# The value product of a retention layer, computed with tokens in the rows of y

## The chip, the cores and the metric

The kernel runs on one core of a Trainium2 chip. The metric is the device time of one launch in microseconds; lower is better. Engines are called as in the profile: PE is TensorE (its matmuls), PEld its weight loads, DVE VectorE, ACT ScalarE, POOL GpSimd, SP the engine that issues DMAs. TensorE multiplies a stationary operand, which a weight load puts into its array, by a moving operand that is streamed through it. In the calls below the order of arguments is (output, stationary, moving): the stationary operand's columns become the output's rows, the moving operand's columns the output's columns.

## The reference

For every sequence of 1,024 tokens (8 of them, 256 features) a retention layer and a quantised feed-forward layer are added to the input. The changed lines lie in the retention layer (`_xpos` is a rotary encoding; 8 heads of 32 features):

```python
xn = _layernorm(x)
Q = _xpos(jnp.einsum('bse,hed->bhsd', X, W_Q))
K = _xpos(jnp.einsum('bse,hed->bhsd', X, W_K), downscale=True)
V = jnp.einsum('bse,hed->bhsd', X, W_V)
scores = jnp.einsum('bhsd,bhtd->bhst', Q, K) * D[None]   # D: causal decay gam**(s-t)
Y = jnp.einsum('bhst,bhtv->bhsv', scores, V)
Yn = ((Y - mu) / jnp.sqrt(var + EPS)).reshape(b, s, h * dv) * gn_weight + gn_bias  # per head
gate = X @ W_G; gate = gate * sigmoid(gate)
retention = gate * Yn @ W_O
# feed-forward: fp4 blocks of 16; silu(xq @ w_gate.T) * (xq @ w_up.T), quantised, @ w_down.T
out = x + retention + ffn
```

## The kernel before

The 8,192 tokens are worked off in 64 tiles of 128 tokens, 8 tiles to a sequence. Within a sequence the scores of a tile reach only the tile's own tokens; what earlier tiles contribute is carried in `state` (K transposed times V, summed up), kept for all tiles but the last of a sequence (`kept(t)`; `later(t)` is true for all but the first).

Every engine runs one instruction stream, written out by hand. `step(i)` is the loop body of each engine, i from -4 to 65; in it the engine works on tile i for the projections and the scores, on tile i-1 for the second half of its feed-forward part and y's norm, on tile i-2 for the last pieces and the output, and on tiles i+1 to i+3 for the layer norm and quantisation of the input. Engines meet only in semaphores, and none overtakes within its own stream. So the code's order in a step is the order in time.

What the change and the prediction touch, by name and line of the profile:

- PE, late in step i: three transposes of `hq` (L883), then for kept tiles `kv`, K transposed times V of tile i (L892, eight small products, one a head), then the value product (L901, eight, one a head, val stationary: 32 columns, probs moving: 128), which fills `b_yT`, features in the rows, tokens in the columns. Then the feed-forward's down product (L908, L912, L913). Ahead of L901, for tiles with a state, `state` times `qT` (L869) starts the same sums. L844 is the product of K and Q that makes the scores, eight heads of 32 rows. fp32 products show two records each, one transpose shows one.
- PE, early in step i+1: the query and key projection (L773 to L775, "bank"), the rest of the down product (L789 to L792), the output product of z (L795, L796: high part of z; L808: its low part), and between them the transposes of yT (L802), which turn y to tokens in the rows. After L808 come the gate and up products, dense and long (L773 to L775, "quad").
- ACT, at the end of step i: the copy of yT out of PSUM (L725), then `h_magic` (L727). In step i+1 the state's copies for kept tiles (L672, four), `zT_hi` (L677), the squares of y (L681), `x_magic`.
- POOL, first in a step: `zT_lo` (L376), the low part of z, which L808 waits for (semaphore `z_low`).
- DVE: the sums of squares (L548), the scaled `y_hat` (L592), and the masked scores `probs` (L600, L603). L544 adds L808's result to the input.

Of the kernel before, what the change touches and what calls it, by code (L numbers as in the profile page):

```python
# [19 lines left out]
G = 2  # L20
# [40 lines left out]
def block_kernel(nc, x, w_q, w_k, w_v, w_g, w_o, gn_w, gn_b, w_gate, w_up, w_down, cos_d, sin_d,  # L61
# [4 lines left out]
    with ExitStack() as ctx:  # L66
        def sb(name, shape, dt=F32):
            return ctx.enter_context(nc.sbuf_tensor(name, shape, dt))

        def sem(name):  # L70
            return ctx.enter_context(nc.semaphore(name))
# [54 lines left out]
        probs = sb("probs", [P, HG, G * P])  # L126
        state_sum = sb("state_sum", [P, G * HD])
        state = sb("state", [P, D])
        yT = sb("yT", [P, D])
        y_sq = sb("y_sq", [P, D])  # L130
        y_hat = sb("y_hat", [P, D])
        u_T = sb("u_T", [P, KD, P])
# [28 lines left out]
        b_kv = bank[3]  # L161
        b_out = bank[4][:, 0:D]
        b_vg = bank[6]
        b_yT = [bank[5][:, 0:P], bank[6][:, 0:P]]
        b_y = b_zT = bank[7]


        w_landed = [sem(f"w_landed{n}") for n in range(len(PARTS))]
# [78 lines left out]
        xT_high = sem("xT_high")  # L247
        affine1 = sem("affine1")
        hT_high1 = sem("hT_high1")
        yT_copy = sem("yT_copy")  # L250
        h_abs = sem("h_abs")


        qk_ready = sem("qk_ready")
        down_l1 = sem("down_l1")
        out_high = sem("out_high")
        y_ready = sem("y_ready")
        out_ready = sem("out_ready")
        gu0_ready = sem("gu0_ready")
        gu1_ready = sem("gu1_ready")  # L260
# [7 lines left out]
        down_h0 = sem("down_h0")  # L268
        h1_turned = sem("h1_turned")
        kv_ready = sem("kv_ready")  # L270
        yT_ready = sem("yT_ready")
        down_l0 = sem("down_l0")
        down_h1 = sem("down_h1")

        def exists(t):
            return 0 <= t < TILES
# [18 lines left out]
        def heads(ap):  # L295
            return ap.rearrange("p (h d) -> p h d", d=HD)
# [4 lines left out]
        def tiles(ap):  # L301
            return ap.rearrange("p (k c) -> p k c", c=P)

        def spread(ap, k=BLOCK):
            return ap.unsqueeze(2).broadcast_to([P, ap.shape[1], k])
# [129 lines left out]
        def _(dve):  # L435
# [68 lines left out]
            def step(i):  # L504
# [84 lines left out]
                if exists(i - 1):  # L589
                    t = i - 1  # L590
                    dve.wait_ge(rstd_ready, t + 4)
                    dve.tensor_tensor(heads(y_hat[:]), heads(b_y[:, 0:D]), spread(rstd[:, 1:], HD), ALU.mult).then_inc(y_normed, 1)  # L592
                if exists(i):
                    t = i
                    dve.wait_ge(h_peak, t + 1)
# [67 lines left out]
        def _(act):  # L663
            def step(i):
                if exists(i - 1) and kept(i - 1):
                    t = i - 1
                    if t == 0:
                        act.wait_ge(cleared, 3)
                    act.wait_ge(kv_add, kept_upto(t))
                    for r in range(HG):  # L670
                        rows = slice(r * HD, (r + 1) * HD)
                        ins = act.activation(tiles(state[:])[rows, :, rows], heads(state_sum[:])[rows], ACT.Copy)  # L672
                    ins.then_inc(state_copy, 1)
                if exists(i - 2):
                    t = i - 2
                    act.wait_ge(z_mul, t + 1)
                    act.activation(zT_hi[:], zT[:], ACT.Copy).then_inc(z_high, 1)  # L677
                if exists(i - 1):
                    t = i - 1
                    act.wait_ge(y_ready, t + 1)  # L680
                    act.activation(y_sq[:], b_y[:, 0:D], ACT.Square, scale=HD ** -0.5).then_inc(squared, 1)  # L681
                if exists(i + 1):
                    t = i + 1
                    act.wait_ge(x_divided, t + 1)
                    act.activation(x_magic[:], x_quot[:], ACT.Abs, scale=GROW).then_inc(x_abs, 1)  # L685
                if exists(i):
                    t = i
                    act.wait_ge(gu0_ready, t + 1)
                    act.activation(silu[:, 0, :], b_gate[0][:, 0:FH], ACT.Silu).then_inc(silu0_done, 1)  # L689
                    act.wait_ge(gu1_ready, t + 1)  # L690
                    act.activation(silu[:, 1, :], b_gate[1][:, 0:FH], ACT.Silu).then_inc(silu1_done, 1)  # L691
                    act.wait_ge(qk_turned, t + 1)
                    act.activation(qT[:], tiles(b_qkT[:, 0:D]), ACT.Copy).then_inc(q_copy, 1)
                    act.activation(kT[:], tiles(b_qkT[:, D:2 * D]), ACT.Copy).then_inc(k_copy, 1)
                    act.wait_ge(vg_ready, t + 1)
                    act.activation(val[:], b_vg[:, 0:D], ACT.Copy).then_inc(v_copy, 1)
                if exists(i + 2):
                    t = i + 2
                    act.wait_ge(x_shifted, t + 1)
                    act.activation(xn[:, t % 2, :], x_in[:, t % SLOTS, :], ACT.Identity,  # L700
                                   bias=x_shift[:], scale=rstd[:, 0:1]).then_inc(x_normed, 1)
                if exists(i):
                    t = i
                    act.activation(gate[:, t % 2, :], b_vg[:, D:2 * D], ACT.Silu).then_inc(gate_silu, 1)
                if exists(i - 1):
                    t = i - 1
                    act.wait_ge(h0_turned, t + 1)
                    act.activation(hT_hi[:, 0:3, :], tiles(b_hT[0][:, 0:3 * P]), ACT.Copy).then_inc(hT_high0, 1)
                    act.wait_ge(z_turned, t + 1)
                    act.activation(u_T[:, 0, :], b_zT[:, 0:P], ACT.Identity,  # L710
                                   bias=gnb[:, 0:1], scale=gnw[:, 0:1]).then_inc(affine0, 1)
                if exists(i + 1):
                    t = i + 1
                    act.wait_ge(x_turned, t + 1)
                    act.activation(xT_hi[:], tiles(b_xT), ACT.Copy).then_inc(xT_high, 1)
                if exists(i - 1):
                    t = i - 1
                    act.activation(u_T[:, 1, :], b_zT[:, P:2 * P], ACT.Identity,
                                   bias=gnb[:, 1:2], scale=gnw[:, 1:2]).then_inc(affine1, 1)
                    act.wait_ge(h1_turned, t + 1)  # L720
                    act.activation(hT_hi[:, 3:6, :], tiles(b_hT[1][:, 0:3 * P]), ACT.Copy).then_inc(hT_high1, 1)
                if exists(i):
                    t = i
                    act.wait_ge(yT_ready, t + 1)
                    act.activation(tiles(yT[:]), quad[:, 3:5, 0:P], ACT.Copy).then_inc(yT_copy, 1)  # L725
                    act.wait_ge(h_divided, t + 1)
                    act.activation(h_magic[:], h_quot[:], ACT.Abs, scale=GROW).then_inc(h_abs, 1)  # L727

# [42 lines left out]
        def _(pe):  # L771
# [5 lines left out]
            def step(i):  # L777
# [7 lines left out]
                if exists(i - 2):  # L785
# [9 lines left out]
                        pe.matmul(b_out, zT_hi[:, k], w_out_hi[:, k], start=False, stop=False)  # L795
                        ins = pe.matmul(b_out, zT_hi[:, k], w_out_lo[:, k], start=False, stop=False)  # L796
                    ins.then_inc(out_high, 1)
                if exists(i - 1):
                    t = i - 1
                    pe.wait_ge(yT_copy, t + 1)  # L800
                    for g in range(G):
                        ins = pe.transpose(b_y[:, g * P:(g + 1) * P], yT[:, g * P:(g + 1) * P], ident[:])  # L802
                    ins.then_inc(y_ready, 1)
                if exists(i - 2):
                    t = i - 2
                    pe.wait_ge(z_low, t + 1)
                    for k in range(KD):
                        ins = pe.matmul(b_out, zT_lo[:, k], w_out_hi[:, k], start=False, stop=k == KD - 1)  # L808
                    ins.then_inc(out_ready, 1)
                if exists(i):  # L810
# [9 lines left out]
                        pe.wait_ge(w_low, sum(PART_GROUPS[:-1]))  # L820
                    if t >= 2:
                        pe.wait_ge(summed, t - 1)
                    for dst, c in ((b_gate[1], FH), (b_up[1], F + FH)):
                        for k in range(KD):
                            ins = product(dst[:, 0:FH], xT_hi[:, KD:], xT_lo[:, KD:], w_gu_hi[:, :, c:c + FH],
                                          w_gu_lo[:, :, c:c + FH], k, start=k == 0, stop=k == KD - 1)
# [37 lines left out]
                if exists(i) and later(i):  # L864
                    t = i
                    pe.wait_ge(masked1, t + 1)
                    pe.wait_ge(gate_silu, t + 1)
                    for g in range(G):
                        ins = pe.matmul(b_yT[g], state[:, g * P:(g + 1) * P], qT[:, g, :], start=True, stop=False)  # L869
                    ins.then_inc(st_ready, 1)  # L870
                if exists(i - 1):
                    t = i - 1
# [22 lines left out]
                if exists(i):  # L895
                    t = i
                    pe.wait_ge(gate_silu, t + 1)
                    for g in range(G):
                        for r in range(HG):
                            rows, head = slice(r * HD, (r + 1) * HD), (g * HG + r) * HD  # L900
                            ins = pe.matmul(b_yT[g][rows, :], val[:, head:head + HD], probs[:, r, g * P:(g + 1) * P],  # L901
                                            start=t % CHUNKS == 0, stop=True)
                    ins.then_inc(yT_ready, 1)
                if exists(i - 1):
                    t = i - 1
                    pe.wait_ge(hT_low0, t + 1)
# [71 lines left out]
```

## Time and profile before

| | |
|---|---|
| median of 3 runs | 949.45 us (949.44 to 951.26) |
| the profiled execution's own time | 948.74 us |
| its span (first to last instruction) | 946.9 us |
| PE busy | 888.8 us, 94% |
| DVE busy | 895.9 us, 95% |
| ACT busy | 528.5 us, 56% |
| POOL busy | 443.7 us, 47% |

The span is the profiled execution from its first to its last instruction; 1.8 us of its time lie outside. Two engines are busy nearly throughout. Since matmuls are pipelined, a busy PE says little by itself: how far apart its instructions start has to be read from the timeline. A wait names the engine's instruction that stood idle and who released it.

### The profile page before, as it was taken

Reading aid. Unit: us, or ns where it says so; the run is one execution under the profiler, and the core shown is the slowest. Engines: PE = TensorE matmul, PEld = TensorE weight load, DVE = VectorE, ACT = ScalarE, POOL = GpSimd, SP = SyncE. Lnnn points to the kernel's source line nnn. Section 1 sums busy time; section 2 is a strip of 40 time slices with the busy share of each in tenths; the row PEclk is TensorE's granted clock in tenths of the full one; section 3 lists DMA queues with packets and bytes.
Section 4 is the critical chain, followed back from the end, with each engine's and each line's share of the span. In section 5 each row is a group of like instructions: output and inputs, shape, how many; then the busy total and the mean of one; then the engine's idle time right before and its main releaser. Section 6 shows DMA issues by size and latency. Waiting matters only on the chain.

```text
span 946.9 us, 21085 instructions
## 1 busy us (share of the span) xinstructions
PE 888.8 (94%) x8258; PEld 798.1 (84%) x8258; DVE 895.9 (95%) x2220; ACT 528.5 (56%) x1331; POOL 443.7 (47%) x343
## 2 busy tenths in 40 slices
PE   0169999999999999999999999999999999999997
PEld 0158988898989899889988998998899889989986
DVE  5899999999999999999999999999999999999995
ACT  1345565556556655665555566556655655565553
POOL 3564544553454445444544444554445344444543
PEclk9999999999999999999999999999999999999999
DMA  9000000000000000000000000000000000000000
GB/s 281 40 1 12 24 12 24 23 24 13 24 23 19 18 24 24 12 24 24 24 12 24 24 19 17 23 24 12 24 23 24 14 24 23 18 19 24 12 7 17
DMA packets 28259, 24.95 MB, mean 26 GB/s; under 512 B 9088, under 2 KB 27648, under 8 KB 27904
## 3 DMA queue, kind: packets, MB, share of 16 engines
q1 hardware_dynamic: 20224, 18.95, 6.5%
q10 hardware_dynamic: 7936, 4.66, 1.7%
q8 instruction: 65, 1.06, 0.5%
q14 instruction: 34, 0.28, 0.1%
HBM read 15.21 MB, written 8.39 MB: 25 GB/s over the span
## 4 chain that ended last, share of the span: by engine, by line
PE 91%; DVE 5%; POOL 2%; ACT 1%; DMA 0%; issue 0%; SPq 0%; DVEq 0%; POOLq 0%
PE quad L775 11%; PE quad L773 11%; PE quad L774 11%; PE quad L844 4%; PE quad L908 4%; PE bank L850 3%; PE bank L855 3%; PE quad L901 3%; PE bank L774 3%; PE bank L775 3%; PE bank L773 3%; PE bank L830 3%; PE bank L862 3%; PE quad L869 3%; PE quad L878 2%; PE quad L877 2%
## 5 line engine op out<-in xcount | busy, mean ns | idle before, releaser
L392 POOL TENSOR_TENSOR h_quot<-h,h_inv 128x704 f32<-128x704 f32 x64 | 88.9, 1389 | 266.2 <-DVE h_inv L607 266.2
L388 POOL TENSOR_TENSOR rstd<-var_eps,power 128x9 f32<-128x9 f32 x67 | 158.0, 2358 | 38.6 <-DVE var_eps L557 38.5
L774 PE MATMUL quad<-w_gu_lo,xT_hi 128*128 128x352 f32 x512 | 165.1, 322 | 0.0
L775 PE MATMUL quad<-w_gu_hi,xT_lo 128*128 128x352 f32 x512 | 165.1, 322 | 0.0
L773 PE MATMUL quad<-w_gu_hi,xT_hi 128*128 128x352 f32 x512 | 165.0, 322 | 0.0
L376 POOL TENSOR_TENSOR zT_lo<-zT,zT_hi 128x256 fp32r<-128x256 f32 x64 | 51.8, 809 | 164.6 <-ACT zT_hi L677 164.6
L775 PEld LDWEIGHTS quad<-w_gu_hi,xT_lo 128*128 128x128 f32 x512 | 96.2, 188 | 0.0
L773 PEld LDWEIGHTS quad<-w_gu_hi,xT_hi 128*128 128x128 f32 x512 | 96.2, 188 | 0.0
L774 PEld LDWEIGHTS quad<-w_gu_lo,xT_hi 128*128 128x128 f32 x512 | 96.1, 188 | 0.0
L384 POOL TENSOR_TENSOR qk<-qk_cos,qk_sin 128x512 f32<-128x512 f32 x64 | 82.9, 1295 | 7.1 <-DVE qk_sin L531 6.5
L689 ACT ACTIVATE silu<-quad 128x352 f32<-128x352 f32 x64 | 29.8, 465 | 92.2 <-PE quad L775 92.2
L691 ACT ACTIVATE silu<-quad 128x352 f32<-128x352 f32 x64 | 29.7, 463 | 92.2 <-PE quad L775 92.2
L681 ACT ACTIVATE y_sq<-bank 128x256 f32<-128x256 f32 x64 | 24.6, 385 | 76.2 <-PE bank L802 76.2
L672 ACT ACTIVATE state<-state_sum 32x64 f32<-32x64 f32 x224 | 56.1, 250 | 2.0
L588 DVE TENSOR_REDUCE h_max<-h 128x44 f32<-128x704 f32 x64 | 56.7, 886 | 0.1
L568 DVE TENSOR_TENSOR hq<-h_grid,h_scale 128x704 f32<-128x704 f16 x64 | 56.3, 880 | 0.1
L560 DVE SCALAR_TENSOR_TENSOR h_grid<-h_magic,h_diff 128x704 f16<-128x704 bf16 x64 | 56.1, 877 | 0.0
L773 PE MATMUL quad<-w_qkvg_hi,xT_hi 128*128 128x512 f32 x128 | 55.8, 436 | 0.0
L518 DVE SCALAR_TENSOR_TENSOR h_diff<-h_magic,h_quot 128x704 f32<-128x704 bf16 x64 | 54.8, 856 | 0.8 <-ACT h_magic L727 0.7
L844 PEld LDWEIGHTS quad<-qT,kT 32*128 32x128 f32 x1024 | 34.3, 185 | 24.5 <-issue 24.5
L877 PE MATMUL quad<-w_dn_hi,hT_hi 128*128 128x256 f32 x192 | 54.0, 310 | 0.0
L552 DVE SCALAR_TENSOR_TENSOR x_diff<-x_magic,x_quot 128x256 f32<-128x256 bf16 x64 | 51.1, 799 | 0.8 <-ACT x_magic L685 0.8
(147 smaller groups left out, 2849.5 us busy)
## 6 DMA issues: line engine op xcount, KB each, us to landing
x_in<-in_L_attn_X_dram SPq DMA_DIRECT2D x64, 128.0 KB, 2.1
out_dram<-y_out SPq DMA_DIRECT2D x64, 128.0 KB, 1.7
sin<-const_sin_dram ACTq DMA_DIRECT2D x1, 2048.0 KB, 11.1
cos<-const_cos_dram ACTq DMA_DIRECT2D x1, 1024.0 KB, 6.4
raw<-in_L_ffn_w_down_dram SPq DMA_DIRECT2D x2, 352.0 KB, 4.0
raw<-in_L_ffn_w_gate_dram SPq DMA_DIRECT2D x1, 512.0 KB, 3.9
raw<-in_L_ffn_w_up_dram SPq DMA_DIRECT2D x1, 384.0 KB, 5.4
w_qkvg<-in_L_attn_W_Q_dram ACTq DMA_DIRECT2D x2, 128.0 KB, 5.0
```

Source lines behind the costliest of these rows:

```text
L384: pool.tensor_tensor(qk[:], qk_cos[:], qk_sin[:], ALU.add).then_inc(rope_add, 1)
L388: pool.tensor_tensor(rstd[:], var_eps[:], power[:], ALU.pow).then_inc(rstd_ready, 1)
L392: pool.tensor_tensor(blocks(h_quot[:]), blocks(h[:]), spread(h_inv[:]), ALU.mult).then_inc(h_divided, 1)
L560: dve.scalar_tensor_tensor(h_grid[:], h_magic[:], LEAST, h_diff[:], ALU.max, ALU.subtract).then_inc(h_gridded, 1)
L568: dve.tensor_tensor(blocks(hq[:, 0:F]), blocks(h_grid[:]), spread(h_scale[:]), ALU.mult)
L588: dve.tensor_reduce(h_max[:], blocks(h[:]), AX_X, ALU.max, apply_absolute_value=True).then_inc(h_peak, 1)
L672: ins = act.activation(tiles(state[:])[rows, :, rows], heads(state_sum[:])[rows], ACT.Copy)
L773: pe.matmul(out, hi[:, k], w_hi[:, k], start=start, stop=False)
L774: pe.matmul(out, hi[:, k], w_lo[:, k], start=False, stop=False)
L775: return pe.matmul(out, lo[:, k], w_hi[:, k], start=False, stop=stop)
L844: ins = pe.matmul(quad[:, r, g * P:(g + 1) * P], kT[rows, g, :], qT[rows, g, :], start=True, stop=True)
L877: pe.matmul(b_out, hT_hi[:, k], w_dn_hi[:, k], start=k == 0, stop=False)
```

## The change

The value product L901 changes its operands' places: the masked scores of a head, `probs` (128 keys by 128 queries), become the stationary operand, and `val` (128 keys by 32 features) the moving one, so the output has tokens in the rows and the head's 32 features in the columns. The state's product L869 changes places too (`qT` stationary, `state` moving; both are 128x128). ACT's copy L725 then writes y as the norm wants it, in SBUF. The two transposes of yT (L802) and their semaphore go; the squares and `y_hat` read the copy in SBUF instead of PSUM. In a sequence's first tile, where no state product starts the sum, the first head's product does it. The second half of the gate and up products waits for the copy explicitly, since it writes over bank 5. Operands stay fp32.

```diff
-        yT = sb("yT", [P, D])
+        y = sb("y", [P, D])
...
-        b_yT = [bank[5][:, 0:P], bank[6][:, 0:P]]
-        b_y = b_zT = bank[7]
+        b_yg = [bank[5][:, 0:P], bank[6][:, 0:P]]
+        b_zT = bank[7]
...
-                    dve.tensor_tensor(heads(y_hat[:]), heads(b_y[:, 0:D]), spread(rstd[:, 1:], HD), ALU.mult).then_inc(y_normed, 1)
+                    dve.tensor_tensor(heads(y_hat[:]), heads(y[:]), spread(rstd[:, 1:], HD), ALU.mult).then_inc(y_normed, 1)
...
-                    act.wait_ge(y_ready, t + 1)
-                    act.activation(y_sq[:], b_y[:, 0:D], ACT.Square, scale=HD ** -0.5).then_inc(squared, 1)
+                    act.wait_ge(y_copy, t + 1)
+                    act.activation(y_sq[:], y[:], ACT.Square, scale=HD ** -0.5).then_inc(squared, 1)
...
-                    act.wait_ge(yT_ready, t + 1)
-                    act.activation(tiles(yT[:]), quad[:, 3:5, 0:P], ACT.Copy).then_inc(yT_copy, 1)
+                    act.wait_ge(y_ready, t + 1)
+                    act.activation(tiles(y[:]), quad[:, 3:5, 0:P], ACT.Copy).then_inc(y_copy, 1)
...
-                if exists(i - 1):
-                    t = i - 1
-                    pe.wait_ge(yT_copy, t + 1)
-                    for g in range(G):
-                        ins = pe.transpose(b_y[:, g * P:(g + 1) * P], yT[:, g * P:(g + 1) * P], ident[:])
-                    ins.then_inc(y_ready, 1)
-                if exists(i - 2):
-                    t = i - 2
                     pe.wait_ge(z_low, t + 1)
...
                         pe.wait_ge(summed, t - 1)
+                    if t >= 1:
+                        pe.wait_ge(y_copy, t)
...
-                        ins = pe.matmul(b_yT[g], state[:, g * P:(g + 1) * P], qT[:, g, :], start=True, stop=False)
+                        ins = pe.matmul(b_yg[g], qT[:, g, :], state[:, g * P:(g + 1) * P], start=True, stop=False)
...
-                            rows, head = slice(r * HD, (r + 1) * HD), (g * HG + r) * HD
-                            ins = pe.matmul(b_yT[g][rows, :], val[:, head:head + HD], probs[:, r, g * P:(g + 1) * P],
-                                            start=t % CHUNKS == 0, stop=True)
-                    ins.then_inc(yT_ready, 1)
+                            head = slice((g * HG + r) * HD, (g * HG + r + 1) * HD)
+                            ins = pe.matmul(b_yg[g][:, r * HD:(r + 1) * HD], probs[:, r, g * P:(g + 1) * P], val[:, head],
+                                            start=t % CHUNKS == 0 and r == 0, stop=r == HG - 1)
+                    ins.then_inc(y_ready, 1)
```

The rows that follow give PE's instructions in program order (line, operation, output<-operands, shape of the output, what it waits for). The first place is the end of a step, on PE, for a tile with a state, before:

```order
L883 MATMUL quad<-ident,hq 128x128 [waits masked0]
L883 MATMUL quad<-ident,hq 128x128 x2
L892 MATMUL quad<-val,qk 32x32 [waits masked0,v_copy]
L892 MATMUL quad<-val,qk 32x32 x7
L901 MATMUL quad<-probs,val 32x128 [waits gate_silu]
L901 MATMUL quad<-probs,val 32x128 x7
L908 MATMUL quad<-w_dn_hi,hT_lo 128x256 [waits hT_low0]
L908 MATMUL quad<-w_dn_hi,hT_lo 128x256 x2
```

The same place of the changed kernel, whose line numbers are lower by 7 here:

```order
L876 MATMUL quad<-ident,hq 128x128 [waits masked0]
L876 MATMUL quad<-ident,hq 128x128 x2
L885 MATMUL quad<-val,qk 32x32 [waits masked0,v_copy]
L885 MATMUL quad<-val,qk 32x32 x7
L894 MATMUL quad<-val,probs 128x32 [waits gate_silu]
L894 MATMUL quad<-val,probs 128x32 x7
L901 MATMUL quad<-w_dn_hi,hT_lo 128x256 [waits hT_low0]
L901 MATMUL quad<-w_dn_hi,hT_lo 128x256 x2
```

Nothing moved there; the output's shape went from 32x128 to 128x32. The second place is the next step's first part, on PE, from the output product of z to the gate product, before:

```order
L795 MATMUL quad<-w_out_hi,zT_hi 128x256 [waits z_high]
L796 MATMUL quad<-w_out_lo,zT_hi 128x256
L795 MATMUL quad<-w_out_hi,zT_hi 128x256
L796 MATMUL quad<-w_out_lo,zT_hi 128x256
L802 MATMUL bank<-ident,yT 128x128 [waits yT_copy]
L802 MATMUL bank<-ident,yT 128x128
L808 MATMUL quad<-w_out_hi,zT_lo 128x256 [waits z_low]
L808 MATMUL quad<-w_out_hi,zT_lo 128x256
L773 MATMUL quad<-w_gu_hi,xT_hi 128x352 [waits kv_add]
```

And of the changed kernel (one line lower at its start, nine at L808):

```order
L794 MATMUL quad<-w_out_hi,zT_hi 128x256 [waits z_high]
L795 MATMUL quad<-w_out_lo,zT_hi 128x256
L794 MATMUL quad<-w_out_hi,zT_hi 128x256
L795 MATMUL quad<-w_out_lo,zT_hi 128x256
L799 MATMUL quad<-w_out_hi,zT_lo 128x256 [waits z_low]
L799 MATMUL quad<-w_out_hi,zT_lo 128x256
L772 MATMUL quad<-w_gu_hi,xT_hi 128x352 [waits kv_add]
```

The two transposes between the high and the low part of z's product are gone, so the instruction that waits for `z_low` comes directly behind the high part.

## Rows read from the trace of the kernel before

**Rows 1.** The page: busy time of each engine, granted clock in 40 slices, chain by engine.
```profile
PE 888.8 (94%) x8258; PEld 798.1 (84%) x8258; DVE 895.9 (95%) x2220; ACT 528.5 (56%) x1331; POOL 443.7 (47%) x343
...
PEclk9999999999999999999999999999999999999999
...
PE 91%; DVE 5%; POOL 2%; ACT 1%; DMA 0%; issue 0%; SPq 0%; DVEq 0%; POOLq 0%
```

**Rows 2.** The waits: engine, line, for whom; us in total, times, longest us.
```profile
ACT y_sq L681 <- PE bank L802: 76.2, 63, 2.2
...
PEld quad L908 <- issue: 12.5, 63, 0.2
```

**Rows 3.** Timeline around tile 33: start us, us, engine, line, operation, count [idle before].
```profile
519.62 0.49 PE L883 MATMUL quad<-ident,hq 128*128 128x128 f32 x3
...
520.04 0.33 PE L892 MATMUL quad<-val,qk 128*32 128x32 f32 x16
...
520.16 0.38 PEld L901 LDWEIGHTS quad<-probs,val 128*32 128x32 f32 x16
520.19 0.62 PE L901 MATMUL quad<-probs,val 128*32 128x128 f32 x16
...
520.74 0.41 PEld L908 LDWEIGHTS quad<-w_dn_hi,hT_lo 128*128 128x128 f32 x3 [0.20 <-issue]
...
520.88 0.39 ACT L725 ACTIVATE yT<-quad 128x256 f32<-128x256 f32 x1 [0.24 <-PE quad L901]
...
521.16 0.78 ACT L727 ACTIVATE h_magic<-h_quot 128x704 bf16<-128x704 f32 x1
...
521.84 1.04 ACT L672 ACTIVATE state<-state_sum 32x64 f32<-32x64 f32 x4
...
522.90 0.42 ACT L677 ACTIVATE zT_hi<-zT 128x256 fp32r<-128x256 f32 x1
...
523.40 0.74 POOL L376 TENSOR_TENSOR zT_lo<-zT,zT_hi 128x256 fp32r<-128x256 f32 x1 [2.76 <-ACT zT_hi L677]
...
523.87 0.28 PE L796 MATMUL quad<-w_out_lo,zT_hi 128*128 128x256 f32 x1
...
523.99 0.38 PE L802 MATMUL bank<-ident,yT 128*128 128x128 f32 x2
...
524.19 0.30 PEld L808 LDWEIGHTS quad<-w_out_hi,zT_lo 128*128 128x128 f32 x2
```

**Rows 4.** Timeline of the same stretch around tile 31, the last of its sequence.
```profile
492.55 0.49 PE L883 MATMUL quad<-ident,hq 128*128 128x128 f32 x3
...
492.97 0.65 PE L901 MATMUL quad<-probs,val 128*32 128x128 f32 x16
...
493.55 0.41 PEld L908 LDWEIGHTS quad<-w_dn_hi,hT_lo 128*128 128x128 f32 x3 [0.20 <-issue]
...
495.13 1.32 POOL L376 TENSOR_TENSOR zT_lo<-zT,zT_hi 128x256 fp32r<-128x256 f32 x1 [1.55 <-ACT zT_hi L677]
...
496.93 0.30 PEld L808 LDWEIGHTS quad<-w_out_hi,zT_lo 128*128 128x128 f32 x2
```

**Rows 5.** Timeline, weight loads alone, of three lines around tile 33.
```profile
516.53 0.54 PEld L844 LDWEIGHTS quad<-qT,kT 32*128 32x128 f32 x16 [0.36 <-issue]
...
518.35 0.53 PEld L869 LDWEIGHTS quad<-qT,state 128*128 128x128 f32 x4
...
520.04 0.22 PEld L892 LDWEIGHTS quad<-val,qk 128*32 128x32 f32 x16 [0.17 <-issue]
```

**Rows 6.** Groups by line and form, PE matmuls: busy us, mean ns of one.
```profile
L901 PE MATMUL quad<-probs,val 128*32 128x128 f32 x1024 | 40.1, 274 | 0.0
...
L892 PE MATMUL quad<-val,qk 128*32 128x32 f32 x896 | 18.6, 201 | 1.1 <-DVE probs L603 1.1
```

**Rows 7.** Groups by line and form, PE weight loads: busy us, mean ns of one.
```profile
L869 PEld LDWEIGHTS quad<-qT,state 128*128 128x128 f32 x224 | 29.4, 191 | 0.1
...
L901 PEld LDWEIGHTS quad<-probs,val 128*32 128x32 f32 x1024 | 24.5, 111 | 1.3 <-issue 1.3
```

More of the change, by code:

```diff
@@ L249, in block_kernel @@
         hT_high1 = sem("hT_high1")
-        yT_copy = sem("yT_copy")
+        y_copy = sem("y_copy")
         h_abs = sem("h_abs")
@@ L256, in block_kernel @@
         out_high = sem("out_high")
-        y_ready = sem("y_ready")
         out_ready = sem("out_ready")
@@ L270, in block_kernel @@
         kv_ready = sem("kv_ready")
-        yT_ready = sem("yT_ready")
+        y_ready = sem("y_ready")
         down_l0 = sem("down_l0")
```

## The prediction

> **What bounds the kernel now.** I began with the page: PE and DVE are both busy for some 95% of the span, the clock is granted in full in every slice, and the chain that ended last is 91% on PE [rows 1]. So what PE starts later, the end gets later, unless a wait absorbs it. The waits show hardly any of PE's but gaps of 0.2 us ahead of L908, 63 times, put down to "issue" [rows 2]: nothing released them. The timeline shows why PE is nonetheless not alone. After the value product L901 (last end 520.19 + 0.62 = 520.81) ACT works in one stretch: the copy of yT, h_magic, four copies of the state, zT_hi, up to 523.32; then POOL makes zT_lo, up to 524.14; and L808's weight load starts at 524.19 [rows 3]. PE had started its second transpose of L802 at 523.99 + 0.38 - 0.27 = 524.10 and would have been free to load then: it waits 0.09 us for `z_low` already. So for each tile with a state there are two loops through L808: PE's own instructions, and L901's end, then ACT, then POOL. The second is the longer one, by that 0.09 us. For the last tile of a sequence the state's copies are missing; there POOL is done at 496.45 and L808 loads only at 496.93 [rows 4]: PE alone binds.
>
> **The gap of 0.2 us.** The last matmul of L901 starts at 520.81 - 0.27 = 520.54, L908's load at 520.74 [rows 3]. L883's last starts at 519.62 + 0.49 - 0.27 = 519.84, L892's load at 520.04 (0.17 us idle ahead of it) [rows 3, 5]. Between L892 and L901 there is none: their loads start at 520.04 and 520.16. The array's shape tells them apart: 128*128, 128*32, 128*32, 128*128. A change of shape costs some 0.20 us from the last matmul's start to the next load. The Trainium skill, TensorEngine Tiling, section Tiling Modes, says that changing the tiling mode drains the engine; by that rule the trace agrees.
>
> **The new value product.** Before: 16 records (each fp32 product has two) in 0.62 us; they start (0.62 - 0.27) / 15 = 23 ns apart, since four heads lie side by side in the array, 32 columns each, and run abreast [rows 3]. After: each head takes all 128 columns, nothing runs abreast, and 16 loads of 128 columns must pass, each before a stream of only 32 columns. No row shows this pairing, so I bound the spacing. The nearest for the load is L869, fp32, whole array: loads (0.53 - 0.19) / 3 = 113 ns apart [rows 5], but it also streams 128 columns, which could be what spaces them. That the load itself takes so long: one lasts 191 ns with 128 columns and 111 ns with 32 [rows 7], 80 ns for 96 columns, so 128 take about 107 ns of a port, the rest being latency. L844's loads start in packs of four over four row groups, (0.54 - 0.19) / 3 = 0.12 us a pack [rows 5]; each row group takes a 128-column load as often as that, not oftener. Upper bounds: load and stream one after the other, 27 ns more (the stream of 32 columns, a quarter of 107); or nothing overlaps, the load's full 191 ns. Lower bounds: stream-bound, as in L892, whose 16 loads of 32 columns take (0.22 - 0.11) / 15 = 7 ns each and thus about 30 ns in each of four column groups [rows 5, 7]. I take 112 ns, since L869 is fp32, of the same shape, and one load behind the other is what the durations say.
>
> The Trainium skill, TensorE: Matmul & The Clock Gate, section LDWEIGHTS, has a load take its columns / 1.2 in ns, whatever its rows: 107 ns. The sum by it would be 5 us lower. The Trainium skill, TensorEngine Tiling, section Performance Considerations, recommends for a moving operand of 64 columns or fewer to swap it with the stationary one and tile by columns, which is the form that this change leaves; it speaks against the change, as the rows do.
>
> **The sum, a tile with a state.** L892's last start is about 520.17 (520.04 + 0.33 - 0.20 [rows 3, 6]). The drain after it is shorter than 0.20 by the shorter stream, 274 - 201 = 73 ns [rows 6]: first load at 520.30. L908 behind such a gap has its second load (0.41 - 0.19) / 2 = 0.11 us after the first; so the first stream is at 520.41 and the sixteenth, 15 x 0.112 = 1.68 us on, at 522.09. It ends 0.20 later, 522.29, against 520.81: **1.48 us later**. ACT's and POOL's chain from there to L808 has no member that the change shortens: its first copy is as large as before, and the squares, which lose their wait for L802 (76.2 us in all [rows 2]), stand behind zT_hi. L808's load thus moves by the same 1.48 us, to 525.67. PE's own way there gets shorter: no drain behind L901 (L908's first stream from 520.85 to 522.20, +1.35) and no transposes (L796's last start goes from 523.87 to 525.22, and L808 could load 0.02 behind it, at 525.24, as L802's does now). PE then waits 0.4 us for z_low in every such tile. What the transposes give back is lost in that wait.
>
> **A last tile of a sequence.** It has no L892: before, L901 comes with a drain ahead and one behind; after, with none. L883's last start 492.77; first new stream 0.11 later, 492.88; last 494.56, end 494.76 against 492.97 + 0.65 = 493.62: +1.14 us. L908's first stream goes from 493.66 to 494.67, +1.01; less two transposes of 0.11 (0.38 - 0.27 [rows 3]) L808's load moves by **0.79 us**, to 497.72. POOL's end, 496.45 + 1.14, plus 0.05 is 497.64: just not binding.
>
> **Elsewhere nothing.** From L808 to the next L901 the orders stay. DVE's work, 895.9 us, fits into a span over 1,000; it falls behind PE nowhere: `h_diff` follows h_magic (+1.48 us at ACT, while DVE has waited), the rotary products follow PE's +1.35. The squares' and y_hat's reads from SBUF stand on engines with over 1 us of new slack per tile; a tenth more in each would not show. The added wait for y_copy stands some 4 us behind the copy.
>
> Tile 0 hides it behind the start-up. That leaves 55 tiles with a state, 55 x 1.48 = 81.4; seven last tiles, 7 x 0.79 = 5.5; tile 63, behind which PE has little to do and z_low decides, 1.14. Together 88 us on 948.74: **1,037 us**. The profiled execution is 0.07% below the median, which is nothing here.
>
> **Rivals.**
> - *The transposes' time comes back after all*, because ACT's and POOL's chain gets faster or the waits are not rigid: L808 moves as PE allows, +1.05 instead of +1.48. 948.7 + 55 x 1.05 + 6 = 1,013. Against it: the order on ACT, and POOL idle for 2.76 us ahead of zT_lo, waiting for zT_hi [rows 3]. 4%.
> - *Load and stream in series*: 27 ns more a record, 0.42 us a tile, 1,064 us. For it: short streams never stood beside whole loads. Against it: L892's 30 ns per column group hold a load and a stream of 27 each. 8%.
> - *The load is hidden, the stream sets the pace*, 32 ns: 15 x 0.08 = 1.2 us less a tile, +0.28 with a state, -0.41 in a last tile: 961 us. With loads half as long (56 ns, records 61 apart), 0.77 us less a tile: 988 us. The rule beside it is in the Trainium skill, TensorE: Matmul & The Clock Gate, Back-to-back issue gap: spacing by the moving operand's columns. Against it: the load's 191 ns. 4%.
> - *Faster*: the sixteen records start as closely as L892's, 7 ns. The last start is then at 520.51, the end 0.1 us earlier than now, and last tiles gain 0.36 and 0.42 us: 948.7 - 55 x 0.1 - 7 x 0.8 = 938 us. It decides from a spacing below 112 - 1480 / 15 = 13 ns. It needs eight heads to run abreast in all columns. 2%.
>
> **How the numbers follow.** My forecast has 82%; by itself 1,030 to 1,045 us (spacing 107 to 118 ns, drains by 0.03). 1,012 takes in the first rival; upward I stop at 1,050, short of the serial one. About 0.2% is what a measurement of this kernel can tell from no change. Slower than by 0.2% is every case but the last, 0.98, of which I leave 0.01 to no change, between the hidden load and the last case; faster has the last case's 0.02.
>
> **What would show it.** Loads of the new product 107 to 118 ns apart, in one row of 16 with nothing abreast; no gap ahead of L908; a wait of PE for zT_lo of about 0.4 us in seven tiles of eight and none in the eighth; ACT's wait ahead of the copy of y 1.4 us longer; DVE idle over 1 us a tile. The forecast is wrong if the sixteen loads take less than 1.5 us or more than 2, or if L808 follows L795 at once.

## The result, and the profile after

The changed kernel takes 1037.07 us (1036.72 to 1037.53) beside 949.89 us of the kernel before on the same chip: 1.092 times as long, 95% interval 1.090 to 1.093. The forecast was 1,037 us.

From the page of the changed kernel, its span, busy times, clock and the chain by engine:

```profile
span 1035.1 us, 20891 instructions
...
PE 974.1 (94%) x8130; PEld 886.4 (86%) x8130; DVE 909.5 (88%) x2220; ACT 525.9 (51%) x1331; POOL 441.6 (43%) x343
...
PEclk9999999999999999999999999999999999999998
...
PE 75%; ACT 13%; POOL 6%; DVE 3%; issue 1%; DMA 0%; SPq 0%; DVEq 0%; POOLq 0%
```

PE's share did not grow, but its busy time did, by 85 us. The chain used to be 91% PE [rows 1]; now ACT and POOL hold 19% of it: they lie between the value product's end and the low part of z's product. DVE, formerly 95% busy, now has 12% to spare. The clock is granted in full as before, but for a little in the last of the 40 slices.

The waits of the changed kernel:

```profile
ACT y L724 <- PE quad L894: 104.4, 64, 2.6
...
DVE h_diff L517 <- ACT h_magic L726: 63.0, 64, 1.7
...
PEld quad L799 <- POOL zT_lo L375: 16.1, 56, 0.7
```

ACT waits 104.4 us for the value product's result. In the kernel before the same wait was:

```profile
ACT yT L725 <- PE quad L901: 14.6, 56, 1.3
```

That is 89.8 us more, 1.4 us a tile. PE's weight load ahead of z's low part (now L799) waits for zT_lo 56 times, 0.29 us each. DVE stands idle 1 us a tile for h_magic, which ACT makes behind the copy of y. The gap of 0.2 us ahead of the down product [rows 2] has no row any more.

The timeline around tile 33, a tile with a state, which answers to [rows 3]:

```profile
565.20 0.49 PE L876 MATMUL quad<-ident,hq 128*128 128x128 f32 x3
...
565.62 0.33 PE L885 MATMUL quad<-val,qk 128*32 128x32 f32 x16
...
565.88 1.86 PEld L894 LDWEIGHTS quad<-val,probs 128*128 128x128 f32 x16
565.88 1.97 PE L894 MATMUL quad<-val,probs 128*128 128x32 f32 x16
...
567.66 0.42 PEld L901 LDWEIGHTS quad<-w_dn_hi,hT_lo 128*128 128x128 f32 x3
...
567.89 0.39 ACT L724 ACTIVATE y<-quad 128x256 f32<-128x256 f32 x1 [1.67 <-PE quad L894]
...
568.17 0.78 ACT L726 ACTIVATE h_magic<-h_quot 128x704 bf16<-128x704 f32 x1
...
568.85 1.04 ACT L671 ACTIVATE state<-state_sum 32x64 f32<-32x64 f32 x4
...
569.91 0.42 ACT L676 ACTIVATE zT_hi<-zT 128x256 fp32r<-128x256 f32 x1
...
570.41 0.73 POOL L375 TENSOR_TENSOR zT_lo<-zT,zT_hi 128x256 fp32r<-128x256 f32 x1 [4.18 <-ACT zT_hi L676]
...
570.84 0.28 PE L795 MATMUL quad<-w_out_lo,zT_hi 128*128 128x256 f32 x1
...
571.19 0.30 PEld L799 LDWEIGHTS quad<-w_out_hi,zT_lo 128*128 128x128 f32 x2 [0.28 <-POOL zT_lo L375]
```

The sixteen loads of the value product L894 take 1.86 us in all and the last of them 0.19, so they start (1.86 - 0.19) / 15 = 0.111 us apart. Count everything from the last hq transpose's start (565.42 here, 519.84 before). The product ends 2.43 us behind that start instead of 0.97; L799's load starts 5.77 us behind it instead of 4.35. The difference is 1.42 us a tile. Behind the last start of L795 (570.84) the load stands still until POOL is done (571.14) and 0.05 us more.

The last tile of a sequence, tile 31, which answers to [rows 4]:

```profile
535.91 0.49 PE L876 MATMUL quad<-ident,hq 128*128 128x128 f32 x3
...
536.24 1.87 PE L894 MATMUL quad<-val,probs 128*128 128x32 f32 x16
...
537.91 0.42 PEld L901 LDWEIGHTS quad<-w_dn_hi,hT_lo 128*128 128x128 f32 x3
...
539.59 1.14 POOL L375 TENSOR_TENSOR zT_lo<-zT,zT_hi 128x256 fp32r<-128x256 f32 x1 [2.65 <-ACT zT_hi L676]
...
541.07 0.31 PEld L799 LDWEIGHTS quad<-w_out_hi,zT_lo 128*128 128x128 f32 x2
```

From the last hq transpose (536.13) to L799 it is 4.94 us instead of 4.16: 0.78 us more. POOL is done at 540.73, 0.34 us ahead of that load, so PE itself is the later one.

All value products of the launch (durations in ns: min, median, max; then first and last start in us; the forms at the end are not needed here):

```profile
L894 PEld LDWEIGHTS quad<-val,probs x1024: 186/192/193, 69.8 to 1018.9; 128*128 128x128 f32 x171
L894 PE MATMUL quad<-val,probs x1024: 194/276/297, 69.8 to 1018.9; 128*128 128x32 f32 x171
```

The first starts at 69.8, the last at 1018.9: 949.1 us. Before, the matmuls' row was:

```profile
L901 PE MATMUL quad<-probs,val x1024: 272/273/297, 68.2 to 931.3; 128*32 128x128 f32 x171
```

That is 863.1 us. So 86 of the 88.2 us between the two profiled executions lie between the first and the last value product; 1.6 lie ahead of them, in the start-up, and 0.6 behind.

### The profile page after: what moved, and what is told of

Same layout as the page of the kernel before. It is cut to its first block, busy times and chain, and to the rows that moved or that the text cites. A ratio compares the mean times of both kernels' runs of the same rounds, so it can differ in the third digit from the quotient of the medians.

```text
span 1035.1 us, 20891 instructions
## 1 busy us (share of the span) xinstructions
PE 974.1 (94%) x8130; PEld 886.4 (86%) x8130; DVE 909.5 (88%) x2220; ACT 525.9 (51%) x1331; POOL 441.6 (43%) x343
## 4 chain that ended last, share of the span: by engine, by line
PE 75%; ACT 13%; POOL 6%; DVE 3%; issue 1%; DMA 0%; SPq 0%; DVEq 0%; POOLq 0%
PE quad L894 12%; PE quad L774 11%; PE quad L773 11%; PE quad L772 11%; ACT state L671 5%; PE quad L837 4%; POOL zT_lo L375 4%; ACT h_magic L726 4%; PE bank L843 3%; PE bank L848 3%; PE quad L799 3%; PE bank L823 3%; PE bank L855 3%; PE quad L862 2%; ACT zT_hi L676 2%; PE quad L870 2%
## 5 line engine op out<-in xcount | busy, mean ns | idle before, releaser
L894 PE MATMUL quad<-val,probs 128*128 128x32 f32 x1024 | 125.4, 277 | 0.0
L894 PEld LDWEIGHTS quad<-val,probs 128*128 128x128 f32 x1024 | 119.1, 191 | 2.3
L517 DVE SCALAR_TENSOR_TENSOR h_diff<-h_magic,h_quot 128x704 f32<-128x704 bf16 x64 | 57.2, 893 | 63.0 <-ACT h_magic L726 63.0
L724 ACT ACTIVATE y<-quad 128x256 f32<-128x256 f32 x64 | 24.6, 384 | 104.4 <-PE quad L894 104.4
L684 ACT ACTIVATE x_magic<-x_quot 128x256 bf16<-128x256 f32 x64 | 26.7, 417 | 78.7 <-POOL x_quot L379 78.7
L527 DVE TENSOR_TENSOR qk_cos<-bank,cos 128x512 f32<-128x512 f32 x64 | 44.3, 692 | 13.0 <-PE bank L774 12.8
```

Source lines behind the costliest of these rows:

```text
L517: dve.scalar_tensor_tensor(h_diff[:], h_magic[:], LEAST, h_quot[:], ALU.max, ALU.subtract).then_inc(h_diffed, 1)
L894: ins = pe.matmul(b_yg[g][:, r * HD:(r + 1) * HD], probs[:, r, g * P:(g + 1) * P], val[:, head], start=t % CHUNKS == 0 and r == 0, stop=r ...
```

## The experiments

My theory has two parts. The cost: sixteen loads of the whole array's 128 columns, one behind the other, set the product's pace. The missing gain: in tiles with a state the way over ACT and POOL to `z_low` decides, so PE's time for the transposes costs the kernel nothing. Rivals: the cost lies in the array's change of shape, in the state's product or in another engine; the transposes were worth their time.

**The idle transposes.** The changed kernel with two transposes at their old place, into a bank where nobody reads them:

```diff
                     ins.then_inc(out_high, 1)
+                if exists(i - 1):
+                    pe.wait_ge(y_copy, i)
+                    for g in range(G):
+                        pe.transpose(b_zT[:, g * P:(g + 1) * P], y[:, g * P:(g + 1) * P], ident[:])
```

> The changed kernel with the two transposes put back at their old place on PE, between the high and the low part of z's product; they turn y into a bank that nobody reads, so their 0.22 us a tile are pure load. If z_low decides when the low part starts in the tiles with a state (PE waits some 0.36 us there), nothing changes in those and only the seven last tiles pay 0.22 us: 1037 to 1040 us. If PE's own instructions decide, all tiles pay: 64 x 0.22 = 14 us more, 1051 us.

Measured: 1037.70 us (1037.58 to 1038.34), ratio 1.0925 (1.091 to 1.094): nothing changed within the interval. From its timeline, POOL, the transposes (L800), and the load of the low part (L805):

```profile
556.34 0.74 POOL L375 TENSOR_TENSOR zT_lo<-zT,zT_hi 128x256 fp32r<-128x256 f32 x1 [3.60 <-ACT zT_hi L676]
...
556.90 0.38 PE L800 MATMUL bank<-ident,y 128*128 128x128 f32 x2
...
557.13 0.30 PEld L805 LDWEIGHTS quad<-w_out_hi,zT_lo 128*128 128x128 f32 x2
```

POOL ends at 557.08, the load starts 0.05 later. The transposes fill the wait for POOL, exactly as they did before the change.

**No transposes in the kernel before.** The value product keeps its old form, and what read y now reads yT (y_hat's edit, not shown, is like that of the squares). PE also gets an explicit wait for yT's copy ahead of the second half of the gate and up products, as in the changed kernel.

```diff
-                    pe.wait_ge(yT_copy, t + 1)
-                    for g in range(G):
-                        ins = pe.transpose(b_y[:, g * P:(g + 1) * P], yT[:, g * P:(g + 1) * P], ident[:])
-                    ins.then_inc(y_ready, 1)
...
-                    act.activation(y_sq[:], b_y[:, 0:D], ACT.Square, scale=HD ** -0.5).then_inc(squared, 1)
+                    act.activation(y_sq[:], yT[:], ACT.Square, scale=HD ** -0.5).then_inc(squared, 1)
```

> The kernel before without its two transposes; the squares and y_hat read yT as it is, so the norm is taken over the wrong numbers (left out: turning y). The value product keeps its old form. If z_low decides, PE waits 0.3 us where the transposes were, and only last tiles gain: 946 to 949 us. If the transposes were worth their time on PE: 949.5 - 14 = 936 us.

Measured: 950.85 us beside 950.07, ratio 1.0011 (1.0002 to 1.0019). 128 transposes, 0.11 us of PE's time each, are gone, and nothing is gained; I had expected 946 to 949 us. Its wait for zT_lo, the whole row of the value product, and PE ahead of the transposes of y_hat (L848), in the step after a sequence's last value product:

```profile
PEld quad L799 <- POOL zT_lo L375: 13.9, 56, 0.6
...
L894 PE MATMUL quad<-probs,val x1024: 272/273/298, 69.4 to 932.5; 128*32 128x128 f32 x171
...
504.85 0.42 DVE L591 TENSOR_TENSOR y_hat<-yT,rstd 128x256 f32<-128x256 f32 x1
505.32 0.20 PEld L848 LDWEIGHTS bank<-ident,y_hat 128*128 128x128 f32 x2 [0.19 <-DVE y_hat L591]
```

Before, the wait for zT_lo had one entry of 0.4 us; now it has 56 of 0.25 us each, which are the transposes' time in another form. From the first value product to the last it is 863.1 us, as before, and each step from one product to the next agrees within 0.03 us: no tile got shorter. The later start-up of this execution, 1.2 us, says nothing of the edit. The 1.5 us that I expected of the seven last tiles did not come either, since in each of these steps PE stands still again, for y_hat: its load starts 0.05 us behind DVE's end. In the kernel before it is so too:

```profile
503.64 0.41 DVE L592 TENSOR_TENSOR y_hat<-bank,rstd 128x256 f32<-128x256 f32 x1
...
504.11 0.20 PEld L855 LDWEIGHTS bank<-ident,y_hat 128*128 128x128 f32 x2
```

y_hat is done at 504.05, the load starts at 504.11. So in one step of eight it is DVE that sets PE's pace.

**128 columns streamed instead of 32.**

```diff
-ins = pe.matmul(b_yg[g][:, r * HD:(r + 1) * HD], probs[:, r, g * P:(g + 1) * P], val[:, head],
+ins = pe.matmul(b_yg[g], probs[:, r, g * P:(g + 1) * P], val[:, g * P:(g + 1) * P],
```

> The changed kernel with 128 columns of val streamed per head instead of 32, into the group's whole 128 output columns (left out: the choice of the head's own features; the heads are summed). Same 16 loads, four times the stream. If the load of 128 columns sets the pace at 112 ns, a stream of 107 ns hides beside it: 16 records stay 112 ns apart, at most 0.08 us a tile more at the end of the last: 1037 to 1043 us. If load and stream come one after the other, each record costs 80 ns more: 64 x 1.28 = 82 us, 1119 us.

Measured: 1041.17 us (1040.78 to 1041.66). The product's loads and matmuls in a tile with a state:

```profile
522.88 1.86 PEld L894 LDWEIGHTS quad<-val,probs 128*128 128x128 f32 x16
522.88 2.05 PE L894 MATMUL quad<-val,probs 128*128 128x128 f32 x16
```

The loads are as far apart as with 32 columns, 0.111 us, and the whole is longer by the last stream alone, 2.05 against 1.97 us. 64 x 0.08 = 5 us; measured are 4.1 more than the changed kernel's 1037.07. Four times the stream costs nothing beside the loads; the two don't run one after the other.

**Half the heads.**

```diff
-                        for r in range(HG):
+                        for r in range(HG // 2):
                             head = slice((g * HG + r) * HD, (g * HG + r + 1) * HD)
```

> The changed kernel with the value product of only two heads in four (left out: the other two of each group); 8 loads of 128 columns a tile instead of 16. If each load costs 112 ns and its end is passed on whole through ACT, POOL and z_low: 63 x 0.89 = 56 us less, 981 us. If DVE or another engine had become the bound in the changed kernel, or the loss came from the change of the array's shape and not from the loads: less than 20 us.

Measured: 979.72 us (979.03 to 979.80), 57.4 us less than the changed kernel. Over 63 tiles that is 0.91 us a tile for eight loads, 0.114 us each, passed on whole. The loads in the first tile of a sequence, and the wait for zT_lo:

```profile
521.55 0.97 PEld L894 LDWEIGHTS quad<-val,probs 128*128 128x128 f32 x8
...
PEld quad L799 <- POOL zT_lo L375: 16.0, 56, 0.7
```

The loads are (0.97 - 0.19) / 7 = 0.111 us apart as before, and the wait is as long as in the changed kernel: both ways to L799 got shorter alike. DVE is no bound at that pace, and the change of shape, which is still there, is not what costs.

**The state's product in the old order.**

```diff
-ins = pe.matmul(b_yg[g], qT[:, g, :], state[:, g * P:(g + 1) * P], start=True, stop=False)
+ins = pe.matmul(b_yg[g], state[:, g * P:(g + 1) * P], qT[:, g, :], start=True, stop=False)
```

> The changed kernel with the state's product in its old order (state stationary, qT moving), so that y gets wrong values from it (changed: the state's part comes in turned over). Both operands are 128 by 128, so nothing changes: 1036 to 1038 us. If the swap of the state's product had a share in the loss, this run is faster than the changed kernel by that share.

Measured: 1037.13 us (1036.72 to 1037.25), beside the changed kernel's 1037.07. The swap of the state's product costs nothing.

**The low part of z's product later.** The loop that waits for `z_low` becomes a function, which is called inside the gate product:

```diff
-                    pe.wait_ge(z_low, t + 1)
-                    for k in range(KD):
-                        ins = pe.matmul(b_out, zT_lo[:, k], w_out_hi[:, k], start=False, stop=k == KD - 1)
-                    ins.then_inc(out_ready, 1)
...
                     for dst, c in ((b_gate[0], 0), (b_up[0], F)):
                         for k in range(KD):
                             ins = product(dst[:, 0:FH], xT_hi[:, KD:], xT_lo[:, KD:], w_gu_hi[:, :, c:c + FH],
                                           w_gu_lo[:, :, c:c + FH], k, start=k == 0, stop=k == KD - 1)
+                            if c == 0 and k == 0:
+                                z_low_part(i - 2)
```

> The changed kernel, complete, with the low part of z's product (the instruction that waits for z_low) moved behind the first three matmuls of the gate product, 0.48 us further on, so that PE works while ACT and POOL finish zT_lo. If the wait for z_low is what keeps the transposes' time from being gained, its 0.36 us come back in 55 tiles: 1037 - 20 = 1017 us, and no wait for zT_lo is left. If another wait stands right behind it (y_hat, x_quant, DVE's y_out late), less than half of that: 1028 us or more.

Measured: 1018.73 us (1018.02 to 1019.02), 18.3 us less than the changed kernel, 0.33 us for each of 55 tiles. Its waits:

```profile
DVE h_diff L517 <- ACT h_magic L726: 63.6, 64, 1.7
...
PEld quad L781 <- POOL zT_lo L375: 0.7, 1, 0.7
```

Of the 56 waits for zT_lo one is left, at the end, behind the last value product, where no gate product follows. DVE still waits for h_magic as long as before (63.0 us in the changed kernel), as it must if that wait hangs on the value product's end and not on PE's wait. So with the wait out of the way, 18 us come back, and the value product's cost stays.

**The same in the kernel before**, behind the first matmul of the gate product instead of the third. (`z_low_part` is the function of the last experiment.)

```diff
+                    pe.matmul(b_gate[0][:, 0:FH], xT_hi[:, KD], w_gu_hi[:, 0, 0:FH], start=True, stop=False)
+                    z_low_part(i - 2)
+                    pe.matmul(b_gate[0][:, 0:FH], xT_hi[:, KD], w_gu_lo[:, 0, 0:FH], start=False, stop=False)
+                    pe.matmul(b_gate[0][:, 0:FH], xT_lo[:, KD], w_gu_hi[:, 0, 0:FH], start=False, stop=False)
                     for dst, c in ((b_gate[0], 0), (b_up[0], F)):
-                        for k in range(KD):
+                        for k in range(1 if c == 0 else 0, KD):
```

> The kernel before, complete, with the low part of z's product moved behind the first matmul of the gate product (0.16 us further on). PE waits some 0.09 us for z_low in 55 tiles there, so at most 5 us: 945 us. DVE, busy 95% of the span, may take it: then no change, 948 to 951 us.

Measured: 945.18 us beside 950.39, ratio 0.9946 (0.9934 to 0.9959). The 0.09 us that L808 waits [rows 3], 55 times, are 5.0 us; 5.2 were gained. It beats the kernel before and the changed one, and so it is what the last forms below have to be measured against.

**No transposes, low part later.** The edits of "No transposes in the kernel before" and of "The low part of z's product later" together.

> The kernel before without its two transposes (left out: turning y, as in the run without transposes alone), and with the low part of z's product behind the first three matmuls of the gate product. Wait and transposes both gone, PE has 0.31 us less in 55 tiles and 0.22 in seven: 950 - 18.6 = 931 us if PE alone decides. If DVE is the next bound, part of it stays out: 936 to 948 us, and DVE is idle less than 0.3 us a tile. No change at all would say that z_low was not what held the transposes' time back.

Measured: 933.91 us (933.68 to 934.44), ratio 0.9828 (0.9815 to 0.9841), 16.5 of 18.6 us. The transposes do have a price on PE, but it is paid out only when the wait behind them is covered. Most of the rest is DVE's: from each sequence's last value product to the next one it is as long as in the kernel before, within 0.02 us (13.36 there), while the other steps got some 0.3 us shorter. PE's waits for y_hat there:

```profile
PEld bank L856 <- DVE y_hat L591: 2.1, 9, 0.6
```

DVE is near its bound elsewhere too. Between 200 and 500 us it is busy for 294.7 of the 300 us, idle 0.24 us a tile, under the 0.3 us that I had named as a sign of it.

**Quarters.** If loads in turn are the cost, loads abreast must cure it, with y's tokens still in the rows:

```diff
-ins = pe.matmul(b_yg[g][:, r * HD:(r + 1) * HD], probs[:, r, g * P:(g + 1) * P], val[:, head],
-                start=t % CHUNKS == 0 and r == 0, stop=r == HG - 1)
+for q in range(0, P, 32):
+    ins = pe.matmul(b_yg[g][q:q + 32, r * HD:(r + 1) * HD], probs[:, r, g * P + q:g * P + q + 32],
+                    val[:, head], start=t % CHUNKS == 0 and r == 0, stop=r == HG - 1)
```

> The changed kernel, complete, with each value product split by tokens into four of 32 columns of probs as stationary operand, each into its own quarter of the output rows: 64 records of 32-column loads, four abreast, in the array shape of the kv product ahead of them. If the loss is the load of the whole array's columns one after the other, it goes: the kv product's pairs start some 9 ns apart (16 in 0.147 us), so 64 take 0.6 us against 1.79; the end comes 0.17 us a tile after that of the kernel before: 950 + 55 x 0.17 = 959 us. If the loss belongs to probs as stationary operand or to tokens in the rows, it stays at 1037 us.

Measured: 956.83 us (956.60 to 957.38), ratio 1.0071 (1.0058 to 1.0083): 80 of the 87 us are gone. The product in the last tile of a sequence, and its loads' group by form (busy us, mean ns of one):

```profile
498.00 0.65 PEld L895 LDWEIGHTS quad<-val,probs 128*32 128x32 f32 x64 [0.17 <-issue]
498.00 0.76 PE L895 MATMUL quad<-val,probs 128*32 128x32 f32 x64
```

```profile
L895 PEld LDWEIGHTS quad<-val,probs 128*32 128x32 f32 x4096 | 44.0, 109 | 1.3 <-issue 1.3
```

64 loads in 0.65 us, on average (0.65 - 0.11) / 63 = 8.6 ns apart, with the same operand stationary, the same output and four times as many instructions. The array's shape is the old 128*32 again, so this run alone does not part the loads' width from the shape; half the heads and the halves below do.

**Quarters, low part later.** Both edits.

> The quarters, and the low part of z's product behind the first three matmuls of the gate product, complete. The wait for z_low is hidden and the transposes' 0.22 us are then really gone from PE: against the run without transposes and with the low part later (934 us) it has 0.16 us more a tile for the product: 944 us; DVE, near its bound there, could add to that, 948 us.

Measured: 941.70 us (940.85 to 942.78) beside 950.27, ratio 0.9911 (0.9897 to 0.9924), 2.3 us better than I expected. It is the fastest of the kernels here that compute everything. Of its 8.6 us, though, the moved low part alone gave 5.2 in the kernel before (945.18 us); the swapped product in quarters adds 3.4: what the removed transposes give back, less the longer product. Its page's busy times and chain, and its one wait for zT_lo, again at the end:

```profile
PE 881.6 (94%) x11202; PEld 803.2 (85%) x11202; DVE 887.5 (94%) x2220; ACT 525.9 (56%) x1331; POOL 442.8 (47%) x343
...
PE 92%; DVE 3%; POOL 3%; ACT 1%; DMA 1%; issue 0%; SPq 0%; DVEq 0%; POOLq 0%
```

```profile
PEld quad L781 <- POOL zT_lo L375: 0.7, 1, 0.7
```

The chain is back at 92% PE, and PE's own busy time is 7 us below that of the kernel before [rows 1].

**Halves.** As the quarters, with 64 columns:

```diff
-for q in range(0, P, 32):
-    ins = pe.matmul(b_yg[g][q:q + 32, r * HD:(r + 1) * HD], probs[:, r, g * P + q:g * P + q + 32],
+for q in range(0, P, 64):
+    ins = pe.matmul(b_yg[g][q:q + 64, r * HD:(r + 1) * HD], probs[:, r, g * P + q:g * P + q + 64],
```

> The changed kernel, complete, with each value product split by tokens into two of 64 columns: 32 records, two abreast. If loads run abreast in separate column groups, each column group takes 16 records of some 58 ns, 0.93 us: an end 0.6 us a tile after that of the kernel before, 950 + 55 x 0.6 + 3 = 986 us. If all loads share one port whatever their columns' group, 32 x 57 ns = 1.8 us, as in the changed kernel: 1037 us or more.

Measured: 984.60 us (984.00 to 984.92). The product in a last tile, and the loads' form:

```profile
509.96 1.01 PEld L895 LDWEIGHTS quad<-val,probs 128*64 128x64 f32 x32 [0.17 <-issue]
509.96 1.13 PE L895 MATMUL quad<-val,probs 128*64 128x32 f32 x32
```

```profile
L895 PEld LDWEIGHTS quad<-val,probs 128*64 128x64 f32 x2048 | 64.9, 138 | 3.6 <-issue 1.3
```

(1.01 - 0.14) / 31 = 28 ns a record, 56 ns in each of the two column groups: the load of 64 columns, in turn within a group and abreast between the groups. In each column group a record takes 111, 56 and 34 ns with 128, 64 and 32 columns to load: half the columns take half the time, a quarter of them somewhat more than a quarter (28 ns). What adds the 6 ns was not tested.

## Why the prediction was right

- **The product's pace.** Taken as 112 ns from the state's product, between bounds of 7 and 191; measured 111, and by half the heads 114. That the load, not the stream, sets it was argued from two durations; the runs with 128 streamed columns and with halves and quarters show it, and half the heads and the halves, both with a switch of the array's shape behind the kv product, leave that switch hardly a share in the loss.
- **The product's end.** Forecast 1.48 us later; measured 2.43 - 0.97 = 1.46. ACT's copy then starts 0.04 us behind it instead of 0.07, and L808's load (now L799's) moves by 1.42. This term was 4% too large, 3 us in 55 tiles.
- **The transposes' gain lost in the wait for z_low.** Forecast a wait of 0.4 us in seven tiles of eight, none in the eighth. Measured: 56 waits, 0.29 us idle each, with PE free some 0.33 us sooner. The wait is 0.1 us shorter than forecast because ACT's and POOL's way moved by 1.42 instead of 1.48 us and PE's own (L795's last start) by 1.39 instead of 1.35. Putting the transposes back costs nothing, taking them from the kernel before gains nothing, and moving the waiting instruction returns 18 us. The first rival (1,013 us) fails for the reason given: the order on ACT is rigid.
- **A last tile.** Forecast 0.79 us, measured 0.78, with the drains as counted: none before and none behind the product. POOL had 0.08 us to spare there by my sum, and has 0.29 (0.34 less the 0.05 from its end to a load), mostly because its zT_lo took 1.14 us instead of 1.32.
- **Elsewhere nothing.** DVE idles 1 us a tile, as forecast, in front of h_diff. That it falls behind PE nowhere is not so: behind each sequence's last tile PE waits for y_hat, in both kernels. In tile 0 the start-up hides less than I took: from its product to the next one it is 1.0 us longer than before, where I had counted zero. That, a start-up 1.6 us longer in this execution, and 0.7 us more than counted from tile 63's product on make up for the 3 us above. The start-up is luck: the first value product starts anywhere from 68.2 to 70.1 us in the executions here, whatever the edit. So the exact hit of 1,037 owes something to errors of both signs; the medians lie 87.2 us apart, where I forecast 88.
- **The serial rival and the hidden load.** The first would be 139 ns a record and 80 ns more with 128 streamed columns, the second 32 or 61 ns; the pace is 111 ns with either stream. The same pace excludes the faster rival. That one needed heads abreast, which the changed form has not; the quarters get something near it, 8.6 ns, by splitting the tokens, and with the low part later they are faster than before. I had not thought of that when I wrote the rival off.

## What to carry to other kernels

Before swapping operands, count the columns that must be loaded, and in how many column groups at a time. With the fp32 operands here a short stream didn't make a whole-array load cheap, while splitting the stationary operand's columns over the array made loads run abreast. Work that is removed in front of a semaphore wait is worth only what is left after the wait; first find work to stand between, then remove. Here both together turned a loss of 9% into a gain of 0.9%, of which 0.5% came from moving the low part alone, without any swap.

## What the runs showed of the hardware

- Pairs of load and matmul with 32 columns each start on average 8.6 ns apart when four column groups take turns, 64 in 0.76 us, although each load lasts 109 ns. That is the pace of the kv product's sixteen, held over four times as many instructions.
- From 128*32 to 128*128, the time from the last matmul's start to the next load goes with the last stream: 0.20 us behind the old value product's 128 columns (520.54 to 520.74), 0.13 us behind the kv product's 32 (its last matmul starts at 565.62 + 0.33 - 0.20 = 565.75, the next load at 565.88).
- The last matmul of the value product takes 0.28 us from its recorded start to its end, against 0.20 for the kv product's with the same 32 columns; their loads take 0.19 and 0.11. The record begins while its own load still runs: it starts at 565.88 + 1.97 - 0.28 = 567.57, the load ends at 565.88 + 1.86 = 567.74. Starts of load-bound matmuls are thus not starts of streams. (The ends of matmuls in the profile are modelled, so the durations count for less here than the starts.)
